# Attention step: Q5, Q4 and Q3 in this order ahead of the second heads, and TensorE's implied waits left out in the loop

## The chip, the cores and the metric

The kernel runs on one core of one Trainium2 chip. The metric is the device time of one execution in microseconds. Engines run at the same time and wait for each other by semaphores: TensorE (PE; its weight loads are shown apart as PEld), VectorE (DVE), ScalarE (ACT), GpSimd (POOL) and SyncE (SP), which issues nearly all DMA transfers.

## The reference: attention over heads, then a gated feed-forward, each with a residual and a layer norm

x has 8 x 1024 rows of 512. The attention mixes the 16 heads of one row with each other; it doesn't mix rows.

```python
q = rope((x @ Wq.T + bq).reshape(B, S, 16, 32))       # k the same way, v without rope
qk = einsum('bshd,bstd->bsht', q, k) / sqrt(32)       # heads against heads, row by row
out = einsum('bsht,bstd->bshd', softmax(qk), v)
out = swapaxes(out, 1, 2).reshape(B, S, E) @ Wo.T + bo
x = layernorm(x + out)
g, u = (x @ gate_w.T) * gate_s, (x @ up_w.T) * up_s   # gate_w, up_w, down_w are -1, 0 or 1
x = layernorm(x + ((silu(g) * u) @ down_w.T) * down_s)
```

## The kernel before

**Units and steps.** The 8192 rows are 64 tiles of 128 rows, taken two at a time: 32 units. First all units go through the attention (to about 760 us), then eight super-steps do the feed-forward. Each fp32 product is three single-pass products of 512 columns (high by high, high by low, low by high): lines 646, 647 and 650 in the helper `three`, which all wide products of the attention go through.

**The seven products of Q and K.** Q and K of a unit's two tiles are made with seven half-size products in place of eight (a Strassen-like scheme): Q1 to Q7, six wide products each. Their sums are gathered partly in PSUM: QK_BANK names the bank of each. Q1, Q6, Q7 and Q4 go one on top of the other into BANK_X; Q2 has BANK_Z; Q5 and then Q3 go into BANK_W, where Q3 adds to what Q5 left. VectorE reads a bank between two such products: `first_sum_of_qk` behind Q1, `second_sum_of_qk` behind Q6, `third_sum_of_qk` behind Q7, `k_of_first` behind Q2, `k_of_second` behind Q4, `q_of_second` (L1614) behind Q5 and `q_of_first` (L1619) behind Q3. Each raises a semaphore (q1_made, q0_made and so on), and the product that writes the bank next waits for it in `block_of_qk`.

**One step of TensorE.** `step(u)` runs for u = 2 by itself and in a loop for u = 3 to 30 (`last_step` is u = 31). It works on three units: Q, K and V of unit u, scores of unit u - 1, and values and output heads of unit u - 2. Its order is Q1, Q2, the small products that weigh the values (L778), the small products of the scores (L791), V of the first tile, Q6, V of the second tile, Q7, output heads of the first tile, Q4, Q5, output heads of the second tile, Q3. V and output heads (`project_v`, `project_heads`) are twelve wide products each. The waits of the two groups of small products are put before the last wide product of Q2 (the argument `ahead`).

**One step of VectorE.** VectorE has its own loop. `begin_step` does `q_of_first` and its transpose `turn_q(.., 0)` (L1634) of the unit before; `rest_of_step` follows the order of TensorE, from `first_sum_of_qk` over `low_of_heads` (L1682), `subtract_top` (L1648, L1651), `add_v_bias`, `scale_prob` (L1664), `turn_prob`, `turn_x1`, to `add_residual` (L1712, L1715), the sums of K and Q and their transposes. The scores of a unit need all four transposes, those of K after ScalarE has spread them (`spread_k`, L1101).

**Other engines.** ScalarE and GpSimd split the next unit's rows and their sums into high and low parts: `high_of_tile(u + 1, 1)` waits for Q4, which reads the same buffer; `high_of_sum` of Q5 waits for Q5. Beside this GpSimd (L1449 to L1454, L1437) and ScalarE prepare one slab of the feed-forward's weights per step. SP's order in a step is: residual rows of unit u - 2 (the second tile's load waits for the residual sum of unit u - 3's second tile, y_done), four stores of the slab before, thirteen loads of the next slab (L455), the values of unit u - 1, and then stores and the next rows.

Of the kernel before, what the change touches and what calls it, by code (L numbers as in the profile page):

```python
# [37 lines left out]
DIRECT = 2  # L38
# [11 lines left out]
def at_least(eng, sem, count):  # L50

    if isinstance(count, int) and count <= 0:
        return
    eng.wait_ge(sem, count)


def post_ln_layer(nc, x_cols, x_rows, rope, w_qkvo, biases, ffn_w, scales, down_s, eye, head_mask, out):
# [25 lines left out]
    with ExitStack() as ctx:  # L83
# [80 lines left out]
        Q1, Q2, Q3, Q4, Q5, Q6, Q7 = range(7)  # L164
# [59 lines left out]
        v_done, v_biased = sem("v_done"), sem("v_biased")  # L224
# [5 lines left out]
        scores_done, max_done, sub_done, exp_done = sem("scores_done"), sem("max_done"), sem("sub_done"), sem("exp_done")  # L230
# [412 lines left out]
        def _(pe):  # L643
# [8 lines left out]
            def inputs_of_tile(m, t):  # L652
                pe.wait_ge(a_hi_done, 2 * m + t + 1)
                if isinstance(m, int) and m == 0:
                    pe.wait_ge(a_lo_first, t + 1)
                else:
                    pe.wait_ge(a_lo_done, 2 * (m - 1) + t + 1)
# [17 lines left out]
            def block_of_qk(q, m, ahead=None):  # L675
                t = {Q1: 0, Q2: 0, Q4: 1}.get(q)
                if t is not None:
                    inputs_of_tile(m, t)
                else:
                    pe.wait_ge(s_hi_done, 4 * (m - DIRECT) + S_ORDER.index(q) + 1)  # L680
                    pe.wait_ge(s_lo_done, 4 * (m - DIRECT) + S_ORDER.index(q) + 1)
                first = isinstance(m, int) and m == DIRECT
                if first:
                    weights_made(q)
                if q == Q1:
                    if first:
                        pe.wait_ge(q0_made, DIRECT)
                    else:
                        pe.wait_ge(k1_made, m)
                elif q == Q2:  # L690
                    if first:
                        pe.wait_ge(q1_made, DIRECT)
                    else:
                        pe.wait_ge(k0_made, m)
                    at_least(pe, y_done, 2 * (m - 3) + 1)
                elif q == Q6:
                    pe.wait_ge(qk_s1_made, m - DIRECT + 1)
                elif q == Q7:
                    pe.wait_ge(qk_u2_made, m - DIRECT + 1)
                elif q == Q4:  # L700
                    pe.wait_ge(qk_u3_made, m - DIRECT + 1)
                elif q == Q5:
                    pe.wait_ge(v_biased, 2 * m + 1)
                    pe.wait_ge(q0_made, m)
                else:
                    pe.wait_ge(q1_made, m + 1)
                hi, lo = operand(q, m)
                w_hi, w_lo = weights_of(q)
                for k in range(KH):
                    last = three(ps_x[QK_BANK[q]][:, :], hi[:, k], lo[:, k], w_hi[:, k], w_lo[:, k],  # L710
                                 k == 0 and q in (Q1, Q2, Q5), k == KH - 1, ahead if k == KH - 1 else None)
                last.then_inc(qk_done[q], 1)

            def project_v(m, t, ahead=None):
                inputs_of_tile(m, t)
                bank = BANK_Y if t else BANK_W
                if isinstance(m, int) and m == 1:
                    bank = BANK_Z if t else BANK_X
                    pe.wait_ge(k1_made if t else k0_made, 1)
                elif isinstance(m, int) and m == DIRECT:  # L720
                    pe.wait_ge(k1_made if t else k0_made, 2)
                elif not isinstance(m, int) or m > DIRECT:
                    pe.wait_ge(v_biased, 2 * (m - 1) + t + 1)
                    if t == 0:
                        pe.wait_ge(q0_made, m)
                    else:
                        pe.wait_ge(y_done, 2 * (m - 3) + 2)
                hi, lo = split_of(m)
                for k in range(KE):
                    if isinstance(m, int) and m == 0:  # L730
                        pe.wait_ge(wv_hi_done, k + 1)
                        pe.wait_ge(wv_lo_done, k + 1)
                    last = three(ps_x[bank][:, :], hi[:, t, k], lo[:, t, k], wv_hi[:, k], wv_lo[:, k],
                                 k == 0, k == KE - 1, ahead if k == KE - 1 else None)
                last.then_inc(v_done, 1)

            def project_heads(m, t):
                ending = isinstance(m, int) and m >= UNITS - 2
                if isinstance(m, int) and m == 0:
                    pe.wait_ge(wo_hi_done, KE)  # L740
                    pe.wait_ge(wo_lo_done, KE)
                by_tile = isinstance(m, int) and m == UNITS - 2
                pe.wait_ge(ahi_done, 2 * m + (t + 1 if by_tile else 2))
                pe.wait_ge(alo_done, 2 * m + (t + 1 if by_tile else 2))
                if ending:
                    pe.wait_ge(y_done, 2 * (m - 1) + (2 if m == UNITS - 2 else t + 1))
                    pe.wait_ge(q0_made, UNITS if t == 1 else UNITS - 1)
                elif t == 0:
                    pe.wait_ge(k0_made, m + 3)
                    at_least(pe, y_done, 2 * (m - 1) + 1)  # L750
                else:
                    pe.wait_ge(v_biased, 2 * (m + 2) + 2)
                    at_least(pe, y_done, 2 * (m - 1) + 2)
                bank = (BANK_Y, BANK_W)[t] if ending else (BANK_Z, BANK_Y)[t]
                for k in range(KE):
                    last = three(ps_x[bank][:, :], aT_hi[:, t, k], aT_lo[:, t, k], wo_hi[:, k], wo_lo[:, k],
                                 k == 0, k == KE - 1)
                last.then_inc(o_done, 1)

            def inputs_of_av(m):  # L760
                pe.wait_ge(spread_done, m + 1)
                pe.wait_ge(v8_loaded, 16 * (m + 1))
                at_least(pe, ahi_done, 2 * m)
                at_least(pe, alo_done, 2 * m)

            def inputs_of_score(m):
                at_least(pe, sub_done, m)
                pe.wait_ge(turned[0], 2 * m + 2)
                pe.wait_ge(k_spread, 2 * m + 2)

# [27 lines left out]
            def step(u):  # L798
                block_of_qk(Q1, u)
                if isinstance(u, int) and u == DIRECT:  # L800
                    block_of_qk(Q2, u, lambda: inputs_of_av(u - 2))
                    weigh_values(u - 2)
                    project_v(u, 0, lambda: inputs_of_score(u - 1))
                    score(u - 1)
                else:
                    block_of_qk(Q2, u, lambda: (inputs_of_av(u - 2), inputs_of_score(u - 1)))
                    weigh_values(u - 2)
                    score(u - 1)
                    project_v(u, 0)
                block_of_qk(Q6, u)  # L810
                project_v(u, 1)
                block_of_qk(Q7, u)
                project_heads(u - 2, 0)
                block_of_qk(Q4, u)
                block_of_qk(Q5, u)
                project_heads(u - 2, 1)
                block_of_qk(Q3, u)

            def last_step(u):
                block_of_qk(Q1, u)  # L820
# [733 lines left out]
        def _(dve):  # L1554
# [172 lines left out]
                   .then_inc(blo_done, 1)  # L1727

            def begin_step(u):
                q_of_first(u - 1)  # L1730
                turn_q(u - 1, 0)

            def rest_of_step(u):
                later = not (isinstance(u, int) and u == DIRECT)
                first_sum_of_qk(u)
                if later:
                    aggregate(u - 3)
                k_of_first(u)
                turn_k(u, 0)
                low_of_heads(u - 2)  # L1740
                subtract_top(u - 1)
                if later:
                    shift_of(u - 3)
                add_v_bias(u, 0)
                second_sum_of_qk(u)
                sums_of_prob(u - 1)
                scale_prob(u - 1)
                add_v_bias(u, 1)
                third_sum_of_qk(u)
                turn_prob(u - 1)  # L1750
                if later:
                    turn_x1(u - 3)
                add_residual(u - 2, (0,))
                k_of_second(u)
                q_of_second(u)
                turn_k(u, 1)
                turn_q(u, 1)
                add_residual(u - 2, (1,))

            def step(u):  # L1760
                begin_step(u)
# [382 lines left out]
```

## Time and profile before

| | |
|---|---|
| median of 3 runs | 1680.69 us (1678.19 to 1681.34) |
| the profiled execution | 1678.94 us, span 1677.2 us |
| PE busy | 1650.0 us, 98% of the span |
| DVE busy | 1316.7 us, 79% |
| ACT busy | 981.9 us, 59% |
| POOL busy | 630.6 us, 38% |
| share of PE on the chain that ended last | 92% |
| granted TensorE clock | 0.998 of 2.4 GHz |

Busy time of PE is modelled from the starts of its products: the length shown for a wide product (0.39 us) overlaps the next one, so distances between starts are what counts. A row of a timeline has the start in us from the span's start, the length, engine, line, operation, what is written and read, and in brackets the idle time of the engine just before with what ended it.

### The profile page before, as it was taken

Reading aid. Unit: us, or ns where it says so; the run is one execution under the profiler, and the core shown is the slowest. Engines: PE = TensorE matmul, PEld = TensorE weight load, DVE = VectorE, ACT = ScalarE, POOL = GpSimd, SP = SyncE. Lnnn points to the kernel's source line nnn. Section 1 sums busy time; section 2 is a strip of 40 time slices with the busy share of each in tenths; the row PEclk is TensorE's granted clock in tenths of the full one; section 3 lists DMA queues with packets and bytes.
Section 4 is the critical chain, followed back from the end, with each engine's and each line's share of the span. In section 5 each row is a group of like instructions: output and inputs, shape, how many; then the busy total and the mean of one; then the engine's idle time right before and its main releaser. Section 6 shows DMA issues by size and latency. Waiting matters only on the chain.

```text
span 1677.2 us, 40834 instructions
## 1 busy us (share of the span) xinstructions
PE 1650.0 (98%) x14958; PEld 1354.0 (81%) x14958; DVE 1316.7 (79%) x1932; ACT 981.9 (59%) x1578; POOL 630.6 (38%) x690
## 2 busy tenths in 40 slices
PE   8899999999999999999999999999999999999997
PEld 6688888888888888886888888888888888888886
DVE  7889999999999999998667676676766666767656
ACT  5666666666666666666454554655645545556453
POOL 7767666676667666643101102011011020110112
PEclk9999999999999999999999999999999999999999
DMA  6677878787777878778744535525445364353351
GB/s 211 153 185 169 186 169 196 173 175 177 184 188 167 189 169 194 175 168 257 246 141 138 164 104 170 164 93 189 153 141 161 101 197 159 103 191 119 113 181 59
DMA packets 438708, 275.53 MB, mean 164 GB/s; under 512 B 257280, under 2 KB 377216, under 8 KB 438656
## 3 DMA queue, kind: packets, MB, share of 16 engines
q1 hardware_dynamic: 438512, 274.61, 60.2%
q8 instruction: 28, 0.46, 0.1%
q10 hardware_dynamic: 144, 0.26, 0.0%
q14 instruction: 24, 0.20, 0.0%
HBM read 181.74 MB, written 93.06 MB: 164 GB/s over the span
## 4 chain that ended last, share of the span: by engine, by line
PE 92%; DVE 2%; SPq 2%; issue 1%; ACT 1%; POOL 1%; DMA 1%; POOLq 0%; DVEq 0%; ACTq 0%
PE ps_x L646 12%; PE ps_x L650 12%; PE ps_x L647 12%; PE ps_s L918 9%; PE ps_s L923 9%; PE ps_x L918 8%; PE ps_x L923 7%; PE ps_x L929 5%; PE ps_x L933 5%; PE ps_s L791 3%; PE ps_a L778 2%; PE ps_a L929 2%; PE ps_a L933 2%; PE ps_s L929 2%; PE ps_s L933 2%
## 5 line engine op out<-in xcount | busy, mean ns | idle before, releaser
L918 PE MATMUL ps_s<-x_hi,slot 128*128 128x512 f32 x672 | 264.6, 394 | 0.4
L923 PE MATMUL ps_s<-x_lo,slot 128*128 128x512 f32 x672 | 262.2, 390 | 0.0
L1531 POOL TENSOR_TENSOR z<-z,xr 128x512 f32<-128x512 f32 x60 | 77.0, 1307 | 480.5 <-DVE z L1907 480.5
L918 PE MATMUL ps_x<-x_hi,slot 128*128 128x512 f32 x560 | 219.5, 392 | 3.5 <-ACT sg L1246 1.9
L923 PE MATMUL ps_x<-x_lo,slot 128*128 128x512 f32 x560 | 218.5, 390 | 0.0
L1101 ACT ACTIVATE kX<-kT 32x512 f32<-32x512 f32 x256 | 161.2, 630 | 63.1 <-DVE kT L1640 45.0
L1841 DVE TENSOR_TENSOR hid<-ps_s,hid 128x512 f32<-128x512 f32 x88 | 60.8, 691 | 122.8 <-ACT hid L1254 122.8
L918 PEld LDWEIGHTS ps_s<-x_hi,slot 128*128 128x128 f32 x672 | 126.4, 188 | 34.8 <-ACT u L1285 4.3
L923 PEld LDWEIGHTS ps_s<-x_lo,slot 128*128 128x128 f32 x672 | 126.4, 188 | 25.3
L929 PE MATMUL ps_x<-wd,h 128*128 128x512 f32 x352 | 137.1, 390 | 0.2 <-DVE h L1882 0.2
L933 PE MATMUL ps_x<-wd,h 128*128 128x512 f32 x352 | 137.0, 389 | 0.0
L1386 POOL TENSOR_TENSOR s_lo<-x_sum,s_hi 128x256 fp32r<-128x256 f32 x120 | 89.1, 743 | 126.6 <-ACT s_hi L1093 126.6
L918 PEld LDWEIGHTS ps_x<-x_hi,slot 128*128 128x128 f32 x560 | 105.4, 188 | 28.5 <-issue 4.2
L923 PEld LDWEIGHTS ps_x<-x_lo,slot 128*128 128x128 f32 x560 | 105.4, 188 | 21.7
L1525 POOL TENSOR_TENSOR rs<-mv,pw 128x4 f32<-128x4 f32 x15 | 21.7, 1445 | 267.0 <-DVE mv L1927 267.0
L1258 ACT ACTIVATE sg<-sg,gu_scale 128x512 f32<-128x512 f32 x88 | 63.7, 723 | 90.7 <-DVE sg L1847 90.7
L646 PE MATMUL ps_x<-wv_hi,a_hi 128*128 128x512 f32 x248 | 100.7, 406 | 7.2 <-DVE a_lo L1563 7.2
L646 PE MATMUL ps_x<-wo_hi,aT_hi 128*128 128x512 f32 x256 | 99.8, 390 | 0.4 <-DVE aT_lo L1688 0.4
L647 PE MATMUL ps_x<-wo_lo,aT_hi 128*128 128x512 f32 x256 | 99.6, 389 | 0.0
L650 PE MATMUL ps_x<-wo_hi,aT_lo 128*128 128x512 f32 x256 | 99.6, 389 | 0.0
L647 PE MATMUL ps_x<-wv_lo,a_hi 128*128 128x512 f32 x248 | 97.2, 392 | 0.0
L650 PE MATMUL ps_x<-wv_hi,a_lo 128*128 128x512 f32 x248 | 97.1, 392 | 0.0
(178 smaller groups left out, 4398.9 us busy)
## 6 DMA issues: line engine op xcount, KB each, us to landing
slot<-gu_hi SPq DMA_DIRECT2D x88, 896.0 KB, 5.1
xc<-x_cols SPq DMA_DIRECT2D x32, 512.0 KB, 3.8
v_rows<-v_in SPq DMA_DIRECT2D x32, 512.0 KB, 2.8
v<-v_rows SPq DMA_DIRECT2D x32, 512.0 KB, 5.2
res<-x_rows SPq DMA_DIRECT2D x64, 256.0 KB, 3.8
x_rows<-x_out SPq DMA_DIRECT2D x32, 512.0 KB, 3.8
x_cols<-x_turn SPq DMA_DIRECT2D x128, 128.0 KB, 2.5
raw<-x_cols SPq DMA_DIRECT2D x64, 256.0 KB, 5.1
```

Of the source, the lines that this page charges most:

```text
L646: pe.matmul(out, hi, w_hi, start=start, stop=False, skip_group_check=True)
L647: pe.matmul(out, hi, w_lo, start=False, stop=False, skip_group_check=True)
L650: return pe.matmul(out, lo, w_hi, start=False, stop=stop, skip_group_check=True)
L918: pe.matmul(out[:, :], slot[:, WEIGHTS[i], cols], x_hi[:, i, k], start=start, stop=False, skip_group_check=True)
L923: last = pe.matmul(out[:, :], slot[:, WEIGHTS[i], cols], x_lo[:, i, k], start=False, stop=stop, skip_group_check=True)
L929: pe.matmul(out[:, :], h_hi[h][:, rows], wd[:, j], start=first, stop=False, skip_group_check=True)
L933: return pe.matmul(out[:, :], h_lo[h][:, rows], wd[:, j], start=False, stop=last, skip_group_check=True)
L1101: last = act.activation(kX[32 * c:32 * c + 32, t, :, c % 2], kT[32 * c:32 * c + 32], ACT.Copy)
L1258: act.activation(sg1[:, j % 2], sg1[:, j % 2], ACT.Silu, scale=gu_scale[:, 0, j:j + 1])\
L1386: pool.tensor_tensor(s_lo[:, i], x_sum[:, i], s_hi[:, i].bitcast(F32), ALU.subtract).then_inc(s_lo_done, 1)
L1531: pool.tensor_tensor(z[:, h, r], z[:, h, r], rows_of_x1(n, h)[:, r], ALU.add).then_inc(z_added[h], 1)
L1841: dve.tensor_tensor(hid2[:, j], bank_y[:, :], hid2[:, j], ALU.add).then_inc(c22_done, 1)
```

## The change

TensorE's step now has Q5, Q4 and Q3 behind the first tile's output heads, and the second tile's output heads last. VectorE's step follows: `q_of_second` comes ahead of `k_of_second`, `q_of_first` and `turn_q(u, 0)` are done in the same step behind `turn_k(u, 1)`, and the second tile's residual sum moves to the beginning of the next step. In the loop some waits of TensorE are left out: those of `project_v(m, 0)` altogether, that for v_biased in `project_v(m, 1)`, and those for the heads' splits and for sub_done in `inputs_of_av` and `inputs_of_score`. Each of these is implied by another wait ahead of it.

```diff
             def project_v(m, t, ahead=None):
-                inputs_of_tile(m, t)
+                in_loop = not isinstance(m, int)
+                if not (in_loop and t == 0):
+                    inputs_of_tile(m, t)
                 bank = BANK_Y if t else BANK_W
...
-                elif not isinstance(m, int) or m > DIRECT:
-                    pe.wait_ge(v_biased, 2 * (m - 1) + t + 1)
-                    if t == 0:
+                elif in_loop or m > DIRECT:
+                    if not in_loop:
+                        pe.wait_ge(v_biased, 2 * (m - 1) + t + 1)
+                    if t == 0 and not in_loop:
                         pe.wait_ge(q0_made, m)
-                    else:
+                    elif t == 1:
                         pe.wait_ge(y_done, 2 * (m - 3) + 2)
...
             def inputs_of_av(m):
                 pe.wait_ge(spread_done, m + 1)
                 pe.wait_ge(v8_loaded, 16 * (m + 1))
-                at_least(pe, ahi_done, 2 * m)
-                at_least(pe, alo_done, 2 * m)
+                if isinstance(m, int):
+                    at_least(pe, ahi_done, 2 * m)
+                    at_least(pe, alo_done, 2 * m)
...
             def inputs_of_score(m):
-                at_least(pe, sub_done, m)
+                if isinstance(m, int):
+                    at_least(pe, sub_done, m)
...
                 project_heads(u - 2, 0)
+                block_of_qk(Q5, u)
                 block_of_qk(Q4, u)
-                block_of_qk(Q5, u)
+                block_of_qk(Q3, u)
                 project_heads(u - 2, 1)
-                block_of_qk(Q3, u)
...
             def begin_step(u):
-                q_of_first(u - 1)
-                turn_q(u - 1, 0)
+                add_residual(u - 3, (1,))
...
                 add_residual(u - 2, (0,))
+                q_of_second(u)
                 k_of_second(u)
-                q_of_second(u)
                 turn_k(u, 1)
+                q_of_first(u)
+                turn_q(u, 0)
                 turn_q(u, 1)
-                add_residual(u - 2, (1,))
```

## Rows read from the trace of the kernel before

**Rows 1.** Chain in order of time (start us, us, engine, tile, line): first and last mark.
```profile
101.85 1.34 PE ps_a L778 x87
...
737.71 1.43 PE ps_a L778 x91
```
**Rows 2.** Waits of 100 to 737 us: who waited for whom, us, times, longest.
```profile
DVE qk_in L1619 <- DVE stats L1715: 17.4, 28, 0.7
...
PEld ps_x L650 <- DVE qT L1634: 6.5, 26, 0.3
```
**Rows 3.** Timeline of PE: one mark, and the end of Q2 with the next.
```profile
290.27 1.43 PE L778 MATMUL ps_a<-pX,v 64*32 64x64 f32 x124
...
313.17 0.39 PE L647 MATMUL ps_x<-wb_lo,a_hi 128*128 128x512 f32 x1
...
313.81 0.40 PE L778 MATMUL ps_a<-pX,v 64*32 64x64 f32 x24
```
**Rows 4.** Timeline of PE: end of Q2 and mark in the last step.
```profile
737.10 0.39 PE L647 MATMUL ps_x<-wb_lo,a_hi 128*128 128x512 f32 x1
737.32 0.39 PE L650 MATMUL ps_x<-wb_hi,a_lo 128*128 128x512 f32 x1
737.64 0.58 PE L778 MATMUL ps_a<-pX,v 64*32 64x64 f32 x36
```
**Rows 5.** Timeline of PE: from small to wide products, in the loop and feed-forward.
```profile
291.55 1.63 PE L791 MATMUL ps_s<-kX,qT 64*32 64x64 f32 x126
293.11 0.50 PE L646 MATMUL ps_x<-wv_hi,a_hi 128*128 128x512 f32 x1
293.44 0.40 PE L647 MATMUL ps_x<-wv_lo,a_hi 128*128 128x512 f32 x1
...
796.85 1.48 PE L778 MATMUL ps_a<-pX,v 64*32 64x64 f32 x128
798.26 0.50 PE L918 MATMUL ps_s<-x_hi,slot 128*128 128x512 f32 x1
```
**Rows 6.** Timeline of PE: first products of Q4 and Q3.
```profile
304.11 0.39 PE L646 MATMUL ps_x<-wb_hi,a_hi 128*128 128x512 f32 x1
...
309.55 0.39 PE L646 MATMUL ps_x<-wb_hi,s_hi 128*128 128x512 f32 x1
```
**Rows 7.** Timeline of DVE: low_of_heads, scale_prob, k_of_second, q_of_second.
```profile
292.51 1.29 DVE L1682 TENSOR_TENSOR aT_lo<-ps_a,aT_hi 128x512 fp32r<-128x512 f32 x2 [0.17 <-ACT aT_hi L1120]
...
299.96 1.42 DVE L1664 TENSOR_TENSOR prob<-prob,over 128x1024 f32<-128x1024 f32 x1
...
306.20 0.67 DVE L1609 TENSOR_TENSOR qk_in<-ps_x,bias 128x512 f32<-128x512 f32 x1
307.02 0.69 DVE L1614 TENSOR_TENSOR qk_in<-ps_x,qk_in 128x512 f32<-128x512 f32 x1 [0.15 <-PE ps_x L650]
```
**Rows 8.** Timeline of all engines: plain_q and the products that waited for it.
```profile
45.15 0.65 DVE L1583 TENSOR_TENSOR qk_in<-ps_x,bias 128x512 f32<-128x512 f32 x1
...
46.24 0.40 PE L647 MATMUL ps_x<-wb_lo,a_hi 128*128 128x512 f32 x1
...
46.48 0.40 PE L650 MATMUL ps_x<-wb_hi,a_lo 128*128 128x512 f32 x1
```
**Rows 9.** Timeline of POOL: the first two sums of a slab.
```profile
299.93 0.37 POOL L1449 TENSOR_TENSOR f_all<-f_all 128x88 f32<-128x88 f32 x1
300.26 1.35 POOL L1450 TENSOR_TENSOR f_all<-f_all 128x88 f32<-128x88 f32 x1
```
**Rows 10.** Timeline of DVE: scale_prob in the last step.
```profile
749.27 1.23 DVE L1664 TENSOR_TENSOR prob<-prob,over 128x1024 f32<-128x1024 f32 x1
```
**Rows 11.** Timeline of SP: the loads of a slab.
```profile
289.67 6.94 SPq L455 DMA_DIRECT2D f_all<-ffn_w  x13
```
**Rows 12.** DMA issues of 286 to 311 us: KB each, us to landing.
```profile
f_all<-ffn_w SPq DMA_DIRECT2D x10, 22.0 KB, 2.1
```
**Rows 13.** Timeline of ACT: spread_k of the second tile.
```profile
308.75 2.56 ACT L1101 ACTIVATE kX<-kT 32x512 f32<-32x512 f32 x4 [1.24 <-DVE kT L1640]
```

## The prediction

> **What bounds the kernel now.** I read the chain of waits in order of time first. In the attention it is TensorE almost alone and repeats with an even period. I call the start of a step's first small product (L778) its mark; a step u counts from its mark to the next one. Of these marks the reader sees one at 101.85 and, 27 steps later, one at 737.71 [rows 1]: (737.71 - 101.85) / 27 = 23.55 us a step. So the change is worth what it takes from or adds to 23.55 us, times 27. Then the waits of the loop [rows 2]. Two lines name the place that the change touches: VectorE stands 17.4 us in 28 waits (0.6 each) before q_of_first (L1619), at its loop's turn, and behind that a weight load of TensorE (L650) waits 6.5 us in 26 waits for turn_q (L1634). Third, TensorE's timeline around that load. Wide products start 0.2265 us apart: 40 of them from 304.11 to 313.17 [rows 6, 3]. In the loop the mark (313.81) stands 0.64 behind the last L647 product (313.17) [rows 3]; in the last step, whose Q2 doesn't wait for turn_q, it is 737.64 - 737.10 = 0.54 [rows 4]. So TensorE loses 0.10 us a step there, though its load waited 0.25, and nothing else in the step stands out: TensorE is otherwise dense.
>
> **What the change takes away.** With q_of_first and both turn_q behind Q3 and ahead of the second heads, scores have their inputs some 2.7 us earlier (12 products of heads x 0.2265), and the load no longer waits: 26 x 0.10 = 2.6 us. That is nearly all that TensorE's timeline of the loop has to give, so the change can't bring more than about 0.16% there.
>
> **The waits left out.** In the loop those of project_v's first half stand between the last small product of the scores and the first wide one. The trace has the same transition with two wait instructions ahead of it and, in the feed-forward, from L778 to L918, with none. The last group of small products ends at 291.55 + 1.63 = 293.18 and the wide one starts at 293.11, 0.07 ahead of that; without waits 796.85 + 1.48 = 798.33 against 798.26, again 0.07 [rows 5]. So they cost nothing now. Bounds: 0 and, had the whole 0.33 to the second wide product instead of 0.2265 been theirs [rows 5], 0.10 a step; I take 0, since the row without waits is the nearest. The others (those of a_hi, heads' splits and sub_done) are issued while TensorE has queued products before it; they cost nothing for the same dense spacing.
>
> **What the change adds.** Q5 and Q3 write the same bank (BANK_W, Q3 on top of Q5's sum), so Q3 waits for q1_made, that is for q_of_second (L1614), which reads Q5's sum. Before, Q4 starts at 304.11 and Q3 at 309.55, 24 products later: six of Q4, six of Q5 and twelve of the heads [rows 6]. Now only Q4's six stand between: Q5 starts where Q4 did, 304.11, and Q3 would start 12 x 0.2265 = 2.72 later, at 306.83.
>
> VectorE can't be that early. From low_of_heads (L1682, 292.51), which waits for ScalarE's copy behind the small products, it works back to back: scores' maximum, probabilities, V, sums, transposes, and the first half's residual. The first of the two k/q sums starts at 306.20 [rows 7], which is 306.20 - 290.27 = 15.93 behind the mark [rows 3]. The change puts q_of_second in this place, whose length is 0.69 [rows 7]: it ends 16.62 behind the mark. From the end of a VectorE sum to TensorE's product I take the plain_q wait of the opening, the same pair of engines with the wait in an instruction of its own: L1583 ends at 45.15 + 0.65 = 45.80, and the third product starts at 46.48, so the first is worth 46.48 - 2 x 0.2265 = 46.03, or 0.23 behind [rows 8]. Q3's first product thus starts 16.85 behind the mark. From there TensorE has 30 dense products (Q3, heads, Q1, Q2): 29 x 0.2265 = 6.57, and 737.64 - 737.32 = 0.32 from the last one to the mark [rows 4]. Sum 16.62 + 0.23 + 6.89 = 23.74 us: a step becomes a ring through VectorE. Against 23.55 this is +0.19, the taken 0.10 already in it: Q3 would stand some 0.29 a step. The ring holds in all 27 steps, since each part starts from the mark: 27 x 0.19 = 5.1 us. Bounds of the wake-up: 0 (a semaphore that costs nothing) and 0.44 (to the second product's start, 46.24 [rows 8]): -0.04 and +0.40 a step.
>
> **What lies beside.** The first residual sum of the second heads' half moves to the next step's start. Behind it SP has the next residual load, four stores of a slab and thirteen loads of the next. The end of those heads moves by Q3's 1.36 against the mark, and by the 0.10 above, so these loads are issued 1.46 later in the step. Now the last is issued at about 289.67 + 6.94 - 0.43 (one issue) = 296.18 [rows 11] and lands 2.1 later [rows 12], 8.0 behind the mark; that becomes 9.5. GpSimd reads the slab from 299.93 on, 9.66 behind [rows 9]. This cover of 0.2 is thin. Where the slab is late, GpSimd's sums slip behind VectorE's scale_prob (L1664). That one takes 1.42 in the loop [rows 7] and starts while GpSimd's L1449 runs, and GpSimd's next sum, 0.37 long by itself, takes 1.35 beside it [rows 9]; in the last step, with GpSimd idle, scale_prob takes 1.23 [rows 10]. So a late slab would shorten the ring by 0.19. I take a quarter of the steps, 7 x 0.19 = 1.3 us (none and all 27 are the bounds: 0 and 5.1). Q4 ends 1.36 later, so k_of_second, turn_k and the copies to kX come later too, but before these ScalarE waits 1.24 for turn_k and ends at 308.75 + 2.56 = 311.31, 2.5 ahead of the mark [rows 13]; the k sum now starts at Q4's end, some 0.6 later than at 306.20, and even the wait of the Q2 load, 0.6 ahead of the mark, is met. If that cover went, TensorE would stand at Q2 as now. VectorE's turn of the loop (0.6) now falls beside transposes already queued, where nothing waits for it.
>
> **The sum.** 5.1 - 1.3 = +3.8 us. The profiled execution took 1678.94, so 1682.7 for such a one; the median of the runs shown is 1.75 above it, 1680.69, which gives 1684.5.
>
> A rule that bears on the 1.3: the Trainium skill, page "SBUF — State Buffer", section "Who interferes with whom", says that a VectorE instruction with two SBUF inputs and a GpSimd instruction that reads SBUF exclude each other for a whole instruction, the first one in going ahead. The trace agrees at this place (1.42 against 1.23, and 1.35 against 0.37). By that rule alone the sum hangs on who is first in each step.
>
> **Rivals.**
> (a) Q3's wait is met in time. It would need VectorE's q_of_second to end 0.29 earlier; then only the 0.10 is left: 26 x 0.10 = -2.6 us, 1678.1. For it: VectorE gets 0.6 a step back at its loop's turn. Against it: that idle time lies ahead of L1682, whose start ScalarE and the small products set, so it doesn't come through. It decides from a stall of under 0.10 at Q3.
> (b) The slab is late in nearly every step, scale_prob falls to 1.23, the ring to 23.55: 0 us, 1680.7. For it: only 0.2 of cover. Against it: at the same issue time three quarters of the loads should still be there.
> (c) The ring is longer: TensorE's sequencer, held at Q3's wait, needs a second wait's wake-up behind it (0.46 in place of 0.23), and no slab is late: 27 x (0.19 + 0.23) = +11 us, 1692 at most; with half of that 1688. For it: Q3 also waits for its split operands. Against it: these have long been made, so they should pass at once.
> (d) The edit has no effect on the clock of the step, being absorbed in queues: within 0.5 us of before. TensorE's dense rows speak against it; it goes with (b).
>
> **How the numbers follow.** Forecast 0.58, own range 1682.5 to 1687; (a) 0.13; (b) with (d) 0.17; (c) 0.12. The range 1680 to 1688 leaves out (a) and the upper part of (c). About 0.2% (3.4 us) is what can be told from no change. Slower by more: 0.46 of the forecast's share and all of (c), 0.58. Within: the rest of the forecast, (b) and half of (a), 0.35. Faster by more: half of (a), where the ends of the attention would add to its 2.6, 0.07.
>
> **What would show it.** In the profile of the changed kernel: marks 23.65 to 23.75 apart; in the waits a weight load of Q3 (L646 in its line) behind VectorE's q_of_second, some 0.3 to 0.45 each, 27 times; no load at L650 behind turn_q; the 0.6 before q_of_first gone; scale_prob at 1.42 in most steps and 1.23 in some; the transition from the scores to project_v unchanged. Marks 23.45 apart and no wait at Q3 would make the forecast wrong.

## The result, and the profile after

The changed kernel takes 1683.24 us (median of 19 runs, 1680.60 to 1687.08) against 1680.32 (19 runs, 1678.19 to 1683.16): ratio 1.0018, 95% interval 1.0012 to 1.0025, thus 2.9 us slower where 3.8 were forecast (1684.5). The profiled execution took 1684.61 us, its span is 1682.8. That is 5.67 above the profiled one of before, about twice the difference of the medians: one lies above its median, the other below. Lines behind the changed helpers moved by 5: L778 is now L783, L1609 is L1614 (k_of_second), L1614 is L1619 (q_of_second), L1619 is L1624 (q_of_first, now in its own step), L1664 is L1669, L1449 is L1454.

The first view divides the attention. Each row is a window between two marks, with its length, then the busy time of each engine with its count, then the granted clock, the share of the DMA engines and GB/s. The windows are the opening (u = 2 and 3), the 27 steps of the loop, the last step up to its first output head's av product, and the rest up to the av product that ends the attention. Before:

```profile
core 0: us, PE busy (x) PEld busy (x) DVE busy (x) ACT busy (x) POOL busy (x), PEclk, DMA share, GB/s
49.72:101.78 52.06, 47.90 (x694) 39.18 (x693) 41.61 (x61) 32.89 (x59) 35.72 (x41) 1.00 0.70 163
101.78:737.64 635.86, 635.86 (x9343) 528.75 (x9342) 584.78 (x839) 415.13 (x702) 431.61 (x513) 1.00 0.78 179
737.64:756.04 18.40, 18.40 (x323) 15.06 (x322) 16.09 (x22) 11.63 (x16) 4.95 (x9) 1.00 0.80 176
756.04:796.85 40.81, 36.72 (x387) 27.51 (x386) 36.16 (x46) 25.83 (x39) 15.32 (x8) 0.96 0.89 256
```

The same view of the kernel after:

```profile
49.73:103.97 54.24, 49.45 (x693) 40.02 (x692) 41.88 (x61) 32.97 (x59) 35.73 (x41) 0.97 0.66 150
103.97:741.61 637.64, 637.33 (x9344) 526.30 (x9343) 582.80 (x839) 412.91 (x702) 431.76 (x514) 1.00 0.77 178
741.61:761.01 19.40, 18.68 (x323) 15.22 (x322) 16.11 (x22) 10.78 (x15) 4.49 (x8) 1.00 0.76 175
761.01:802.54 41.53, 36.74 (x387) 27.47 (x386) 36.89 (x46) 26.59 (x40) 15.57 (x9) 0.96 0.88 257
```

The loop gives 1.78 of the difference, the last step 1.00, the opening 2.18 and the rest 0.72; the feed-forward takes 880.3 in both. Which of these belong to the order of the work and which to one execution, the experiments tell. In the chain of waits, whose marks answer to [rows 1] (start, us, engine, tile, line), the loop is no longer even:

```profile
104.04 1.35 PE ps_a L783 x87
...
151.34 1.35 PE ps_a L783 x87
175.11 1.34 PE ps_a L783 x87
198.68 1.35 PE ps_a L783 x87
...
741.68 1.43 PE ps_a L783 x91
```

From 151.34 to 175.11 is 23.77, from there to 198.68 is 23.57. All 27 steps are of one of these two kinds: 8 of 23.76 or 23.77 and 19 of 23.53 to 23.57. The waits of 100 to 742 us (us, times, longest), against [rows 2]:

```profile
DVE qk_in L1594 <- DVE stats L1720: 7.8, 27, 0.3
PEld ps_x L646 <- issue: 7.6, 27, 0.4
```

The 17.4 us ahead of q_of_first are gone (0.3 a step are left at VectorE's turn, ahead of the first sum), and so is L650's wait for turn_q. New is a weight load at L646, 27 times: Q3's. The profile names no releaser for it. The timeline of a long step (mark 151.28) shows what it waits for (start, length, engine, line, operation, what is written and read):

```profile
160.92 0.38 POOL L1454 TENSOR_TENSOR f_all<-f_all 128x88 f32<-128x88 f32 x1
160.94 1.44 DVE L1669 TENSOR_TENSOR prob<-prob,over 128x1024 f32<-128x1024 f32 x1
161.26 1.36 POOL L1455 TENSOR_TENSOR f_all<-f_all 128x88 f32<-128x88 f32 x1
...
167.21 0.67 DVE L1619 TENSOR_TENSOR qk_in<-ps_x,qk_in 128x512 f32<-128x512 f32 x1
...
167.60 0.39 PE L650 MATMUL ps_x<-wb_hi,a_lo 128*128 128x512 f32 x1
...
168.02 0.47 PE L646 MATMUL ps_x<-wb_hi,s_hi 128*128 128x512 f32 x1
```

And of the short step behind it (mark 175.04):

```profile
184.71 1.23 DVE L1669 TENSOR_TENSOR prob<-prob,over 128x1024 f32<-128x1024 f32 x1
184.98 1.19 POOL L1454 TENSOR_TENSOR f_all<-f_all 128x88 f32<-128x88 f32 x1 [0.24 <-DMA f_all<-ffn_w]
186.13 0.37 POOL L1455 TENSOR_TENSOR f_all<-f_all 128x88 f32<-128x88 f32 x1
...
190.76 0.67 DVE L1619 TENSOR_TENSOR qk_in<-ps_x,qk_in 128x512 f32<-128x512 f32 x1
...
191.36 0.39 PE L650 MATMUL ps_x<-wb_hi,a_lo 128*128 128x512 f32 x1
191.59 0.46 PE L646 MATMUL ps_x<-wb_hi,s_hi 128*128 128x512 f32 x1
```

In the long step GpSimd's first sum of the slab starts 0.02 ahead of scale_prob, which takes 1.44; q_of_second ends at 167.88 and Q3's first product starts 0.14 later, 0.42 behind the product before it. In the short one the slab has not landed when scale_prob starts: scale_prob takes 1.23, and GpSimd's sum takes 1.19 in place of 0.37. Q3 starts 0.23 behind the product before it, and its second product 0.30 behind the first where a dense one is 0.2265 behind; its weight load still stands 0.41 behind the load before it. So both kinds wait there, the short one less. The landings of the trace part the two kinds without an exception: in the 8 long steps the slab has landed 9.59 us behind the mark at the latest, in the 19 short ones 9.62 at the earliest, and scale_prob starts at 9.67 in all 27.

### The profile page after: what moved, and what is told of

Same layout as the page of the kernel before. It is cut to its first block, busy times and chain, and to the rows that moved or that the text cites. A ratio compares the mean times of both kernels' runs of the same rounds, so it can differ in the third digit from the quotient of the medians.

```text
span 1682.8 us, 40749 instructions
## 1 busy us (share of the span) xinstructions
PE 1654.1 (98%) x14958; PEld 1353.3 (80%) x14958; DVE 1315.6 (78%) x1932; ACT 980.1 (58%) x1578; POOL 630.5 (37%) x690
## 4 chain that ended last, share of the span: by engine, by line
PE 91%; POOL 3%; SPq 1%; DVE 1%; issue 1%; DMA 1%; ACT 1%; POOLq 0%; DVEq 0%; ACTq 0%
PE ps_x L646 12%; PE ps_x L650 11%; PE ps_x L647 11%; PE ps_s L923 9%; PE ps_s L928 9%; PE ps_x L923 7%; PE ps_x L928 7%; PE ps_x L934 5%; PE ps_x L938 5%; PE ps_s L796 2%; PE ps_a L783 2%; PE ps_a L934 2%; PE ps_a L938 2%; PE ps_s L934 2%; PE ps_s L938 2%
## 5 line engine op out<-in xcount | busy, mean ns | idle before, releaser
L646 PE MATMUL ps_x<-wv_hi,a_hi 128*128 128x512 f32 x248 | 101.8, 410 | 7.0 <-DVE a_lo L1568 7.0
L1374 POOL TENSOR_TENSOR a_lo<-xc,a_hi 128x512 fp32r<-128x512 f32 x60 | 79.8, 1331 | 72.3 <-ACT a_hi L1089 72.3
L646 PE MATMUL ps_x<-wo_hi,aT_hi 128*128 128x512 f32 x256 | 100.0, 391 | 0.5 <-DVE aT_lo L1693 0.5
L650 PE MATMUL ps_x<-wo_hi,aT_lo 128*128 128x512 f32 x256 | 99.7, 389 | 0.0
L650 PE MATMUL ps_x<-wv_hi,a_lo 128*128 128x512 f32 x248 | 97.8, 395 | 0.0
```

The costliest lines, as they stand in the source:

```text
L646: pe.matmul(out, hi, w_hi, start=start, stop=False, skip_group_check=True)
L650: return pe.matmul(out, lo, w_hi, start=False, stop=stop, skip_group_check=True)
L1374: pool.tensor_tensor(lo, raw_of(m)[:, 2 * t:2 * t + 2], hi.bitcast(F32), ALU.subtract).then_inc(a_lo_done, 1)
```

## The experiments

All numbers are of whole kernels; the table has the median, the ratio to the kernel before on the same chip (its median lay between 1680.3 and 1681.6 there), and the four windows of one profiled execution each (read as above).

| kernel | us | ratio, 95% | opening | loop | last step | rest |
|---|---|---|---|---|---|---|
| before | 1680.32 | 1 | 52.06 | 635.86 | 18.40 | 40.81 |
| e7_before | 1680.93 (one) | | 54.76 | 635.90 | 18.40 | 39.54 |
| e1_waits | 1681.30 | 1.0001 (0.9992 to 1.0010) | 53.17 | 636.26 | 18.49 | 40.67 |
| after | 1683.24 | 1.0018 (1.0012 to 1.0025) | 54.24 | 637.64 | 19.40 | 41.53 |
| e8_after | 1684.47 (one) | | 53.29 | 638.16 | 19.73 | 41.19 |
| e2_order | 1683.38 | 1.0016 (1.0007 to 1.0025) | 53.18 | 636.52 | 18.66 | 40.42 |
| e3_turn | 1679.87 | 0.9992 (0.9983 to 1.0001) | 54.53 | 632.88 | 20.21 | 40.38 |
| e4_store | 1688.72 | 1.0043 (1.0030 to 1.0057) | 55.19 | 642.47 | 18.40 | 39.88 |
| e5_both | 1678.08 | 0.9983 (0.9974 to 0.9992) | 53.34 | 633.78 | 18.64 | 39.49 |
| e6_late | 1703.02 | 1.0126 (1.0110 to 1.0141) | 56.59 | 654.04 | 19.59 | 40.88 |
| e9_wait | 1682.61 | 1.0009 (1.0000 to 1.0018) | 54.86 | 635.28 | 20.08 | 40.98 |
| e10_end | 1683.39 | 1.0012 (1.0003 to 1.0021) | 56.01 | 638.18 | 18.42 | 41.60 |
| e11_best | 1678.94 | 0.9985 (0.9976 to 0.9994) | 54.28 | 633.64 | 18.47 | 41.09 |

**Waits or order: e1_waits and e2_order.** e1_waits has the old order of TensorE and VectorE, with the waits left out; e2_order has the new order with all waits kept.

```diff
 # e1_waits, against the changed kernel (VectorE's order likewise)
-                block_of_qk(Q5, u)
                 block_of_qk(Q4, u)
-                block_of_qk(Q3, u)
+                block_of_qk(Q5, u)
                 project_heads(u - 2, 1)
+                block_of_qk(Q3, u)
...
 # e2_order, against the changed kernel (the other waits likewise)
-                if not (in_loop and t == 0):
-                    inputs_of_tile(m, t)
+                inputs_of_tile(m, t)
...
```

Expected of e1_waits: 

> The old order, with only TensorE's implied waits left out. Ring theory (the cost is Q3's wait for VectorE's q_of_second, which only the new order brings): the marks stay 23.54 to 23.57 us apart in 26 steps, the load of Q2 still stands behind turn_q, and the transition from the scores to project_v keeps its distance (wide product recorded 0.07 before the end of the small ones); time as before, 1680.3, within 1.5 us. Rival (the waits left out change the time by themselves, by TensorE's sequencer or by code that lies elsewhere): marks up to 0.10 closer, or 1 to 3 us more or less outside the loop.

Expected of e2_order: 

> The new order with all waits kept. Ring theory: the same two levels as in the changed kernel, 23.53 to 23.57 where the slab lands later than 9.62 us behind the mark and 23.76 where it lands sooner; with some 9 of 27 steps on the upper level the time is 1683, about +2.9 us over before. Rival (the waits left out cost or give part of the 2.9): a time that lies at least 1.5 us off the changed kernel's.

The old order without the waits is at 1.0001 of before, the new order with them at 1.0016, as the whole change (1.0018). The waits are worth nothing that can be told, and the order is the whole effect as far as these runs can tell.

**Is it a ring through VectorE: e3_turn.** VectorE's turn of x1 (L1706, 1.29 us for two) stands ahead of q_of_second and nothing urgent needs it. Put behind, it makes q_of_second earlier and changes nothing on TensorE.

```diff
-                if later:
-                    turn_x1(u - 3)
                 add_residual(u - 2, (0,))
                 q_of_second(u)
+                if later:
+                    turn_x1(u - 3)
                 k_of_second(u)
```

Expected: 

> The changed kernel, with VectorE's turn_x1 (two transposes, 1.25 us) moved from ahead of the residual sum to behind q_of_second. q_of_second then starts when Q5 is done, about 15.4 us behind the mark, and ends at 16.1. Ring theory: no load of Q3 waits, scale_prob's length no longer matters, all marks are 23.45 apart, as dense as TensorE can be; the loop gives back 0.16 x 27 = 4.4 us against the changed kernel, 1679 in all. Rival (Q3's stall is only where another limit of the step shows, such as SP's later loads): the marks stay near 23.6 and the wait turns up elsewhere.

All 27 steps take 23.44 us, the loop 632.88, 4.8 less than after and 3.0 less than before; the wait at L646 is not in the list. The timeline of its step from 127.90 has Q3's first product 0.22 behind the one before it:

```profile
143.35 0.68 DVE L1619 TENSOR_TENSOR qk_in<-ps_x,qk_in 128x512 f32<-128x512 f32 x1
143.94 1.29 DVE L1706 STREAM_TRANSPOSE x_turn<-x_out 128x512 f32<-128x512 f32 x2
...
144.22 0.39 PE L650 MATMUL ps_x<-wb_hi,a_lo 128*128 128x512 f32 x1
144.44 0.39 PE L646 MATMUL ps_x<-wb_hi,s_hi 128*128 128x512 f32 x1
```

So Q3's wait for q_of_second is what the new order costs in the loop. Without it the order brings the 0.10 a step of [rows 3, 4], as the forecast's first part has it (23.55 - 0.10 = 23.45). The whole kernel (0.9992, an interval that holds 1) can't be told from before: in its profile the last step took 20.21 and the opening 54.53, both longer than in that of before.

**Does the slab's landing decide the length: e4_store, e6_late, e9_wait, e5_both.** e4_store sends the old slab's four stores ahead of the residual loads, so the new slab lands some 1.9 us earlier (7.75 behind the mark in the median, against 9.67 after).

```diff
-                load_residual(s - 2)
                 store_slab(s - 1)
+                load_residual(s - 2)
```

Expected: 

> The changed kernel, with SP's four stores of a slab ahead of the residual loads, so that the slab's loads are issued some 2 us sooner and land about 7.5 us behind the mark in place of 9.6. Ring theory with the shared port: GpSimd's first slab sum is always ahead of VectorE's scale_prob, which takes 1.44 in every step, and all 27 marks are 23.76 apart: 27 x 23.76 = 641.5 in place of 637.6, so some 3.9 us slower than the changed kernel in the loop, if the ends stay. Rival (the two levels come from something else than the slab's landing, and earlier transfers can only help): marks as in the changed kernel or closer, and a time of 1683 or less.

An earlier load made the kernel slower: the loop takes 4.8 us more than after, and 24 of the 27 steps take 23.76 or more. The view of one tile has scale_prob here (count, then shortest, median and longest ns):

```profile
L1669 DVE TENSOR_TENSOR prob<-prob,over x27: 1224/1441/1465, 114.6 to 733.3; 128x1024 f32<-128x1024 f32 x27
```

The same view of the kernel after:

```profile
L1669 DVE TENSOR_TENSOR prob<-prob,over x27: 1224/1226/1441, 113.6 to 727.8; 128x1024 f32<-128x1024 f32 x27
```

Its median is 1.441 in place of 1.226. Ten steps are at 23.79 to 24.14, beyond the 23.76 of a long step, so the loop is 1.0 above the 641.5 expected: there scale_prob mostly starts later too, by up to 0.36. In the two longest the delay begins on TensorE: its small products at the mark come to their end 0.33 to 0.37 later (in the longest with one pause of 0.29 among them), and ScalarE's copy and VectorE's low_of_heads follow. Why they pause is open. In three steps (23.53 to 23.62) scale_prob is short although the slab came early: there GpSimd came to its first sum only 0.02 to 0.05 behind scale_prob's start.

e6_late was to make the slab late in every step, by the load of the values ahead of it.

```diff
-                    load_slab(s)
                     load_v(s - 1)
+                    load_slab(s)
```

Expected: 

> The changed kernel with SyncE's load of v ahead of the load of the slab, so that the slab's issue waits for the av products and the slab lands over 10 us behind the step's first av product in every step. Theory (the two lengths of a step, 23.76 and 23.53 us, are decided by whether the slab lands before or after VectorE's scale_prob starts): all 27 steps at 23.53 to 23.57 us, scale_prob at 1.22 to 1.23 us in all of them, q_of_second's end at 16.4 us behind the step's start; the loop at 635.8 to 636.0 us, 1.7 us less than the profiled run of the changed kernel, and about 1681.5 us in all. Rival (the two lengths come from something else that goes along with the slab's landing): the mix of 23.53 and 23.76 stays, and the time stays at 1683; or the later slab makes GpSimd's sums and the turn of x1 late, and steps grow beyond 23.8 us.

It missed. scale_prob is 1.22 to 1.23 in all steps, as expected, but with the 512 KB of the values ahead of it the slab landed some 5 us later (14.9 behind the mark in the median, against 9.67), and steps grew to as much as 25.4. The waits of 106 to 760 us show how it goes on to TensorE:

```profile
ACT f_hi L1119 <- POOL f_all L1459: 201.8, 27, 9.0
POOL f_all L1454 <- DMA f_all<-ffn_w: 147.5, 27, 6.9
PEld ps_x L650 <- issue: 21.1, 24, 2.0
PE ps_x L650 <- ACT kX L1106: 11.6, 16, 1.6
```

GpSimd waits for the slab and ScalarE for GpSimd, ScalarE's spread of K comes late, and TensorE stands ahead of the scores. So the slab may be a little late, not much. e9_wait keeps the order and puts one wait ahead of the slab, which is over some 1.5 us behind the mark.

```diff
+                    at_least(sp, av_done, weighed(s - 2))
                     load_slab(s)
                     load_v(s - 1)
```

Expected: 

> The changed kernel with one wait added in SyncE's step: the first load of the slab is issued only when the av products (the small products at a step's start) are done, some 1.5 us behind the step's start in place of 0.9, with the loads in their old order. (In e6_late the value load of 512 KB went ahead as well, and the slab came 4 us late.) Theory: every slab then lands behind 9.62 us from the step's start, thus behind VectorE's scale_prob, so all 27 steps are 23.53 to 23.57 us with scale_prob at 1.22 to 1.23 us, Q3's load stands 0.40, Q2's load doesn't wait, and the loop is 635.8 to 636.2 us; the time 1681.5 us, ratio 1.000 to 1.001 to the kernel before. Rival: the two lengths stay mixed (loop 637 to 638 us), or the later slab lengthens the steps at Q2 as in e6_late.

The view of scale_prob in e9_wait:

```profile
L1670 DVE TENSOR_TENSOR prob<-prob,over x27: 1224/1225/1226, 114.2 to 726.0; 128x1024 f32<-128x1024 f32 x27
```

And the window of its loop:

```profile
104.57:739.85 635.28, 635.28 (x9344) 526.38 (x9343) 580.39 (x839) 412.17 (x702) 428.90 (x514) 1.00 0.77 179
```

All 27 steps are short, 23.50 to 23.57, and the loop takes 2.4 us less than after, a little under what was expected. This separates the two lengths: the landing decides, by the order of one GpSimd and one VectorE instruction. The whole kernel came out 1 us above what was expected, with an opening of 54.86 and a last step of 20.08.

e5_both puts e3_turn and the early stores of e4_store (from the second step of the loop on) together. If the early slab costs only through the ring, it is free here.

```diff
+                if s > DIRECT:
+                    store_slab(s - 1)
                 load_residual(s - 2)
-                store_slab(s - 1)
+                if s == DIRECT:
+                    store_slab(s - 1)
```

Expected: 

> The changed kernel with the turn of x1 between q_of_second and k_of_second (as e3_turn) and, in the steps after the first, SyncE's store of the old slab ahead of the loads of the residual, so that the new slab lands about 2 us earlier. Theory (a ring of VectorE's q_of_second, Q3's load and the next step's start sets the step; the slab's landing only decides by 0.2 us through scale_prob): the turn behind q_of_second takes the ring away, so the earlier slab costs nothing here: all 27 steps stay at 23.4 to 23.5 us, scale_prob at 1.44 in all of them, the loop at 633 us, against 23.76 us a step with the same store in the old place (e4_store). The last step's residual comes no later, so the end is as in e4_store (58.3 us from the last step's start to the last av product) or as in the others (59 to 61). Time 1677 to 1680 us, ratio 0.998 to 0.9995. Rival (the early store costs by itself, by its traffic beside the step's loads): steps of 23.6 to 23.8 us again and about 1686 us.

The view of scale_prob in e5_both:

```profile
L1672 DVE TENSOR_TENSOR prob<-prob,over x27: 1224/1402/1698, 113.0 to 723.3; 128x1024 f32<-128x1024 f32 x27
```

And the window of its loop:

```profile
103.33:737.11 633.78, 633.78 (x9344) 529.00 (x9343) 579.94 (x839) 412.73 (x702) 432.21 (x514) 1.00 0.79 180
```

scale_prob is long in most steps, up to 1.70 (in all of them was expected), and every step still takes 23.47. So its length no longer sets the step. The rival, a cost of the stores by themselves, falls but for 0.03 a step. That an early slab is free was tested less: here it landed at 9.39 behind the mark in the median, only 0.3 earlier than after and not 2. Its median time is the lowest of the kernels here.

**The edges: e7_before, e8_after, e10_end.** e7_before and e8_after are each kernel unchanged, profiled once more.

Expected of e7_before: 

> The kernel before, unchanged, for one more profile: how far the stretch from the second to the fourth step (52.1 us in the profile of before) and from the last step's start to the last av product (59.2 us) differ between two executions of one kernel. If the opening's stall in scores on the first pass of the loop differs between executions rather than between orders, 53 us or more is as likely as 52; the loop behind it stays at 635.9 us within 0.3.

Expected of e8_after: 

> The changed kernel, unchanged, for one more profile: whether the steps are again of two lengths, 23.53 and 23.76 us, and how many of the 27 are long (8 in the first profile, 5 in that of e2_order). Theory: again 4 to 12 long ones, each with the slab landing before GpSimd's first sum starts, and the loop at 636.5 to 638.5 us.

e7_before's opening took 54.76, more than the changed kernel's 54.24 and 53.29. In the first pass of the loop TensorE stands in the scores with no releaser, 3.64 us in the profile of before, 4.41 in e7_before and 3.93 in after. Behind this stall TensorE's granted clock is 0.50 in after and 0.52 in e7_before (from 82 to 84 us in each), and 1.00 in the first profile of before: from the scores' resumption to the sixth product of V it takes 84.44 - 81.17 = 3.27 in after and 82.41 - 80.36 = 2.05 in before, so some 1.2 of the 2.18 lie where the clock was lower. The clock fell there in every other profile of either order too. So the opening of the first pair, 2.18 of its 5.67 us, is for the most part a matter of the execution. A smaller part of the order's isn't excluded: the ten profiles with the new order have openings of 53.2 to 56.6, the three with the old one 52.1 to 54.8. e8_after has 18 short steps and 9 of 23.73 to 23.79, much as the first. The last step is longer in the new order: 18.40 to 18.49 in three profiles of the old one, 19.40, 19.73 and 18.66 in three of the new. TensorE's timeline shows where, first of before and then of after:

```profile
742.00 1.64 PE L791 MATMUL ps_s<-kX,qT 64*32 64x64 f32 x128
...
745.96 1.21 PE L796 MATMUL ps_s<-kX,qT 64*32 64x64 f32 x86
747.89 0.73 PE L796 MATMUL ps_s<-kX,qT 64*32 64x64 f32 x42 [0.72 <-issue]
```

The scores of after stop behind 86 of 128 products, at the same product in e8_after (0.98) and e3_turn (1.50). SP's timeline has the stores of the old slab 1.49 ahead of this step's mark, where they were 2.84 ahead, and four loads of raw whose issue takes 8.20 (6.18 before). Its rows, the first of before and the others of after:

```profile
734.80 0.43 SPq L445 DMA_DIRECT2D dn_hi<-f_hi  x1
...
740.12 0.43 SPq L445 DMA_DIRECT2D dn_hi<-f_hi  x1
...
743.60 8.20 SPq L404 DMA_DIRECT2D raw<-x_cols  x4
```

e10_end takes only these stores, of the last step, ahead of its residual loads.

```diff
+                if s == UNITS - 1:
+                    store_slab(s - 1)
                 load_residual(s - 2)
-                store_slab(s - 1)
+                if s < UNITS - 1:
+                    store_slab(s - 1)
```

Expected: 

> The changed kernel, in which only the last step's stores of the old slab go ahead of its two residual loads. Theory (in the new order the second residual load, and behind it these stores, come 1.4 us later against the step's start, and so run beside the last step's own first pass of code and beside the loads of raw, where TensorE stands in the scores for 0.7 to 1.8 us): TensorE's last step from its start to the next av product goes from 19.4 to 19.7 us back to 18.4 to 18.7 as in the kernel before; the loop stays at 636.5 to 638.2 us; about 1 us less than the changed kernel, 1682.3 us, ratio 1.0005 to 1.0015. Rival: the stall there differs from one execution to the next and is not changed by the stores: 19.0 to 20 us, time 1683.3 us.

SP's timeline of e10_end, whose last step has its mark at 743.66:

```profile
736.55 0.48 SPq L445 DMA_DIRECT2D dn_hi<-f_hi  x1
...
745.66 4.67 SPq L404 DMA_DIRECT2D raw<-x_cols  x4
```

TensorE's timeline of the same step, at the scores:

```profile
748.04 1.66 PE L799 MATMUL ps_s<-kX,qT 64*32 64x64 f32 x128
```

The stores now start 7.11 ahead of the mark. The raw loads take 4.67, the 128 products are in one piece, and the last step is back at 18.42. e4_store, e5_both and e11_best, whose stores also went earlier here, have no such stop either (18.40 to 18.64), and of the six profiles with the stores 1.3 to 1.5 ahead of the mark five have it (0.72 to 1.50); the sixth is e2_order (18.66), the only one of them that keeps all waits. In the time of the whole kernel (1.0012, against 1.0018) the 1 us can't be told from nothing, and the rest of the attention didn't get shorter with it.

**A version that beats both: e11_best.** e3_turn and e10_end together.

Expected: 

> e3_turn (turn of x1 between q_of_second and k_of_second) with the last step's stores as in e10_end, the other steps' stores left in their place. Theory: loop of 632.9 to 633.8 us as in e3_turn and e5_both, last step 18.4 to 18.7 us in place of 20.2: 1677.5 to 1679 us, ratio 0.998 to 0.999, as e5_both. Rival (the end isn't changed by the stores): 1680 us as e3_turn.

Its last step takes 18.47 where e3_turn's took 20.21, its loop 633.64, and the whole 1678.94: ratio 0.9985 (0.9976 to 0.9994). e5_both (0.9983) and this one can't be told apart, and both are faster than the kernel before, by 0.15 to 0.17%.

## Why the prediction was right, and what of it was not

**The waits left out cost nothing** that can be told: shown by e1_waits (1.0001, 0.9992 to 1.0010).

**The 0.10 at Q2's load** is real: no such wait is left after, and where nothing else stands in the way (e3_turn) a step takes 23.44, 0.11 less than before.

**The ring** is the mechanism, and its terms are close. q_of_second starts 167.21 - 151.28 = 15.93 behind the mark, as forecast, and ends 16.60 behind it for 16.62. The wake-up was 0.14 for 0.23; from Q3's first product to the next mark it was 175.04 - 168.02 = 7.02 for 6.89; of the 0.13 more, 0.08 is that the first product behind a wait stands 0.31 ahead of the second in place of 0.2265; the rest is spread over the products behind it. Together 23.76 for the forecast 23.74, and 23.53 to 23.57 for 23.55 where the slab is late. Rival (a) fell: it takes an edit on VectorE, as in e3_turn, to meet Q3's wait. Rival (c), a second wake-up, fell with the 0.14, and rival (d), no effect within 0.5 us, with the interval of 1.0012 to 1.0025.

**The mis-sized term is the share of late slabs**: "I take a quarter of the steps", 7 of 27. It was 19 of 27 (18 in e8_after, 22 in e2_order). The slab was forecast at 9.5 behind the mark against GpSimd's 9.66. Its median was 9.67 (9.45 to 10.00 in 27 steps), 1.70 later than before where 1.46 was forecast: the first load's issue came 1.36 later, but the 13 loads take longer to issue, 7.3 in the median for 7.0 before: [rows 11] has 6.94, and a step of after has

```profile
388.79 7.46 SPq L455 DMA_DIRECT2D f_all<-ffn_w  x13
```

So the credit was not 1.3 but about 4 us (19 x 0.21), and scale_prob was 1.44 in some steps and 1.23 in most, the other way round than forecast. Rival (b), the slab late in nearly every step, was nearer to the truth on this term than the forecast. The loop's cost was 1.78 here, and 1.4 between the means of three profiles of each order (637.44 for after, e8_after and e2_order; 636.01 for before, e7_before and e1_waits), not 3.8.

The Trainium skill, page "SBUF — State Buffer", section "Who interferes with whom", says that a VectorE instruction with two SBUF inputs contends with a GpSimd instruction that reads SBUF for a pair of ports that only one holds at a time, and that the order of issue decides which of them waits. The trace agrees that the order decides: with GpSimd 0.02 ahead scale_prob takes 1.44 for 1.23; with scale_prob ahead, GpSimd's sum takes 1.19 for 0.37. That the later one waits for the other's whole length these rows don't show: scale_prob lost 0.21, and GpSimd's sum still ran for 0.36 by its row.

**What the sum left out** is the end. It followed the residual load 1.46 later into each step and asked only for the slab's loads behind it; the last step stood in the sum at nothing. There TensorE's scores pay: 0.83 more between the means of the same three and three profiles (19.26 and 18.43). The rest of the attention adds 0.7 (41.05 and 40.34) and the opening 0.2 (53.57 and 53.33), both within what one kernel differs by from run to run. 1.4 + 0.8 + 0.7 + 0.2 = 3.2 stands beside 2.9 measured. So the forecast time was met in part by luck: the loop cost less than forecast, and an end that the sum had left out made up for it.

What stays open: why the scores stop behind the 86th product of a pass that runs for the first time. It went away in each of the four kernels whose stores came earlier (e4_store, e5_both, e10_end, e11_best, one profile each), and e2_order lacks it with late stores. So the stores' place bears on it but doesn't decide alone; whether the waits left out have a part, and by which way the stores act, is not shown.

## What to carry to other kernels

When work is moved up on the bounding engine, add up the helper's chain from the step's start to its new deadline: here it was late by 0.3 us, and moving two unhurried transposes (1.29 us together) behind the deadline took 4.8 us from the loop. Where a load's landing has less than 0.2 us to spare against an instruction of another engine, forecast both cases with the spread of the landings, not its middle alone. Follow a moved DMA to the last step as well, where other loads wait in its queue.

## What the runs showed of the hardware that was not expected

- A slab that lands a little later makes the step shorter: e9_wait's loop, with one wait more, takes 635.28 against 637.64, and e4_store's, with earlier stores, 642.47. Much later is worse: e6_late's takes 654.04.
- Two instructions whose starts lie 0.02 us apart decide 0.2 us in every step, so that one program runs in two step lengths with nothing between them (23.53 to 23.57 and 23.76 in the first profile of after).
- Behind the stall of the loop's first pass, in which it stood for some 3 to 4 us, TensorE works at the lower of its two levels (1.2 in place of 2.4 GHz) for a time, in either order and in 12 of the 13 profiles; only the first one of before stays at the upper level, behind a stall of 3.64. In e9_wait, whose granted clock was 0.50 from 80 to 86 us, products then start 0.43 apart, as TensorE's timeline shows here, in place of 0.2265.

```profile
82.49 0.63 PE L648 MATMUL ps_x<-wv_lo,a_hi 128*128 128x512 f32 x1
82.92 0.63 PE L651 MATMUL ps_x<-wv_hi,a_lo 128*128 128x512 f32 x1
```
